# The delta rule's token-tile loop written out as straight-line code on TensorE, VectorE, ScalarE and GpSimd

## The reference, cut to what matters

```python
q = q / (norm(q) + EPS); k = k / (norm(k) + EPS)        # 16 heads of 64
alpha = sigmoid(h @ alpha_w + alpha_b); beta = sigmoid(h @ beta_w + beta_b)
def step(s, inp):
    qt, kt, vt, at, bt = inp
    s = s * at[..., None]
    u = einsum('bhd,bhdv->bhv', kt, s)
    s = s + bt[..., None, None] * (kt[..., None] * (vt - u)[..., None, :])
    return (s, einsum('bhdv,bhd->bhv', s, qt))
```

## Time and profile before

| | us |
|---|---|
| median of three runs | 3277.32 |
| lowest and highest of the three | 3269.51, 3278.38 |
| the profiled execution, own time | 3278.78 |
| its span (first to last instruction) | 3277.0 |
| PE busy | 2846.8 (87%) |
| DVE, ACT, POOL busy | 1550.5 (47%), 1069.3 (33%), 510.5 (16%) |
| the eight tiles of the delta rule | about 2351 to 2905 |

### The profile page before, as it was taken

How to read it: one execution, slowest core, us unless ns; L and a number is a source line. 1 busy time by engine, 2 the same in 40 slices (tenths; PEclk the granted TensorE clock), 3 DMA queues, 4 the chain that set the end, 5 groups by cost and what they waited for, 6 DMA issues and landing times. The chain is left out here.

```text
span 3277.0 us, 97385 instructions
## 1 busy us (share of the span) xinstructions
PE 2846.8 (87%) x43492; PEld 1948.6 (59%) x43492; DVE 1550.5 (47%) x2617; ACT 1069.3 (33%) x1482; POOL 510.5 (16%) x430
## 2 busy tenths in 40 slices
PE   7999999999968799989999999998698999877254
PEld 4666666666645566646666666665477777744132
DVE  3535353535445511145454454544554455524987
ACT  2333333333322121124434344343345444421111
POOL 2333333333312200010000000000011111100000
PEclk8999999999975599989999999998799999988577
DMA  2101110111000001021111111110100000010000
GB/s 78 38 27 38 27 37 27 34 30 32 12 12 0 17 36 38 26 99 37 30 40 27 37 32 32 38 27 30 44 3 4 3 3 3 4 40 29 0 0 13
DMA packets 48769, 88.92 MB, mean 27 GB/s; under 512 B 8640, under 2 KB 43264, under 8 KB 46976
## 3 DMA queue, kind: packets, MB, share of 16 engines
q1 hardware_dynamic: 48384, 82.96, 8.3%
HBM read 81.90 MB, written 1.05 MB: 25 GB/s over the span
## 5 line engine op out<-in xcount | busy, mean ns | idle before, releaser
L525 DVE TENSOR_REDUCE x_mx<-banks 128x2 f32<-128x800 f32 (+1 forms) x512 | 507.0, 993 | 306.3 <-PE banks L640 218.1
L726 PE MATMUL banks<-x_wv,x_cT 128*128 128x256 f32 (+1 forms) x1664 | 467.5, 404 | 24.1 <-DVE x_nmb L530 21.1
L584 PE MATMUL banks<-x_cT,x_wk 128*128 128x400 f32 (+1 forms) x1024 | 364.1, 511 | 17.6 <-DMA x_cT<-in_ctx 17.6
L726 PEld LDWEIGHTS banks<-x_wv,x_cT 128*128 128x128 f32 (+1 forms) x1664 | 279.8, 186 | 146.0 <-issue 76.3
L433 ACT ACTIVATE x_PT<-banks,x_kbs 128x1024 f32<-128x1024 f32 (+1 forms) x208 | 231.5, 1113 | 377.2 <-PE banks L692 377.2
L433 ACT ACTIVATE x_PT<-banks 128x1024 f32<-128x1024 f32 (+1 forms) x208 | 212.8, 1023 | 430.1 <-PE banks L692 358.4
L692 PE MATMUL banks<-x_qbd,x_kT 32*128 32x128 f32 x6656 | 294.7, 274 | 0.0
L584 PEld LDWEIGHTS banks<-x_cT,x_wk 128*128 128x128 f32 x1024 | 193.3, 192 | 163.6 <-issue 27.8
L678 PE MATMUL banks<-x_PT,x_V 128*32 128x64 f32 x13312 | 272.1, 222 | 20.7 <-ACT x_PT L433 20.7
L692 PEld LDWEIGHTS banks<-x_qbd,x_kT 32*128 32x128 f32 x6656 | 253.7, 183 | 0.0
L678 PEld LDWEIGHTS banks<-x_PT,x_V 128*32 128x32 f32 x13312 | 204.9, 109 | 73.7 <-ACT x_PT L433 25.8
(11 more groups left out here) (319 smaller groups left out, 4111.0 us busy)
## 6 DMA issues: line engine op xcount, KB each, us to landing
x_cT<-in_ctx SPq DMA_DIRECT2D x96, 400.0 KB, 3.7
x_cT<-in_ctx SPq DMA_DIRECT2D x32, 401.0 KB, 3.6
e_wu<-in_mo_up SPq DMA_DIRECT2D x9, 512.0 KB, 3.7
e_wd<-in_mo_down SPq DMA_DIRECT2D x9, 512.0 KB, 4.5
x_mrow<-in_mask_row SPq DMA_DIRECT2D x1, 3202.0 KB, 11.5
g_w<-in_db_w SPq DMA_DIRECT2D x3, 1024.0 KB, 7.8
d_wqk<-in_db_qk SPq DMA_DIRECT2D x1, 2048.0 KB, 7.4
f_wgu<-in_fp_gu SPq DMA_DIRECT2D x1, 1536.0 KB, 6.4
```

What stands on the lines that cost most here:

```text
L525: dve.reduce_max(mx[:, H0[k]:H0[k] + 3:2, kb], g.PS[:, first:first + 2, 0:KBS[kb]], AXX).then_inc(max_read, 1)
L584: last = pe.matmul(PJ[pb][:, 0:KBS[k]], wk[:, c, gg, :], cT[:, (p + 1) % 2, c, KB0[k]:KB0[k] + KBS[k]], start=c == 0, stop=c == KC - 1)
L726: last = pe.matmul(PJ[pb][0:CHK[c], 0:D], cT[:, p, cc, 128 * c:128 * c + CHK[c]], wv[:, cc, :], start=cc == 0, stop=cc == KC - 1)
```

## The change

The four `with loop(...)` statements of the delta rule become Python loops. On PE, DVE and ACT the six passes (i = 0 to 5) are written out as tiles 1 to 6, on POOL the seven passes as tiles 0 to 6. The tile's number is then a constant everywhere: in every wait's count, and in the few slices that are picked by the tile (`bass.ds(t, 1)` of `gate`, `beta` and `XN`, and `bass.ds(128 * t, 128)` of `hcT`). The order of the instructions on each engine, their shapes, buffers and semaphores stay as they are.

```diff
@@ -1685,7 +1685,7 @@
             next_tile(0)
-            with loop(nc, pool, NT - 1) as t:
+            for t in range(NT - 1):
                 tile(t, False)
             tile(NT - 1, True)
@@ -1812,7 +1812,7 @@
             levels(0, False, True)
-            with loop(nc, act, NT - 2) as i:
+            for i in range(NT - 2):
                 levels(i + 1, True, True)
             levels(NT - 1, True, False)
@@ -1967,7 +1967,7 @@
             levels(0, False, True)
-            with loop(nc, dve, NT - 2) as i:
+            for i in range(NT - 2):
                 levels(i + 1, True, True)
             levels(NT - 1, True, False)
@@ -2167,7 +2167,7 @@
             levels(0, False, True)
-            with loop(nc, pe, NT - 2) as i:
+            for i in range(NT - 2):
                 levels(i + 1, True, True)
             levels(NT - 1, True, False)
```

## The result

The changed kernel takes 3268.32 us (median of 20 runs, 3261.54 to 3276.99), the kernel before 3275.97 us (20 runs on the same chips): 7.7 us less, a ratio of 0.998 with a 95% interval of 0.9971 to 0.9988. That is inside the 0.3% which I had called no change, and clear of zero.

The account below looks back on a forecast made before the run. PE's instruction stream was taken to set the pace, with missing instruction packets from level 2 on. Terms -2.8 - 1.6 - 2.1 = -6.5 us took 3277.3 to 3270.8 us; range 3264 to 3284.

Parts of the forecast that it names:

- the exit's: PE's fall-through from the loop into tile 7: its 2.06 us stop goes when written out, -2.1 us; 0 if it moves.
- The long stretch: PE from level 2 to L2036, tiles 1 to 6: 31.31 us falls to tile 0's 30.85, -2.8 us in all.
- The stretch ahead: PE from the q projection to level 2: cheaper waits kept, 17.47 to 17.20 us a tile, -1.6 us in all.
- 3. and 4.: Value projection to next tile's transposes, and a tile's first 14 us: nothing taken for either.
- 6.: DVE, ACT and POOL lose register instructions and branch, but their work stays under PE: nothing; +3 us if one stalled.
- the signs for tiles: Profile after: tile starts 67.2 to 67.5 us apart and 13 to 14 instruction packets per tile.
- Rival B: Saved waits kept in full, 2.1 us per tile x 6 + 2.1 = 14.7 us, 3262.6 us; chance 0.08.
- Rival C: Written-out code gets packets at tile 7's slower pace: long stretch +10.2 us, +6.5 in all, 3283.8 us; chance 0.15.
- Rival D: Long stretch gains nothing, the passes' mean being raised by two slow ones: -3.7 us, 3273.6 us; chance 0.22.

Follow-up runs that it names:

- PE alone: Kernel before with only PE's six passes written out; DVE, ACT and POOL keep their loops: 3270.36 us against 3275.30, ratio 0.9984.
- the folded one: Changed kernel with a hardware loop of a single pass around PE's six tiles, its counter folded to a constant: 3267.96 us, ratio 0.9977 to the kernel before.
- the shifted one: Changed kernel with 128 semaphore counts on PE ahead of the delta rule, moving later code half a packet: 3275.41 us against 3271.17 before, ratio 1.0011.
- The two passes with register waits: Changed kernel, but PE loops twice over three written-out tiles, with tile numbers from a register: 3289.65 us against 3281.58 for the kernel before, ratio 1.0021.
- the run without the hint: Kernel before with the branch hint left out of PE's loop (`hint_back_edge=False`): 3284.50 us, ratio 1.0027.
- doubled waits: Changed kernel with every PE wait in levels 2 to 4 made twice: 3284.03 us, ratio 1.002 to the kernel before.
- the shifted loops: Kernel before, loops kept, with 128 semaphore counts on PE ahead of the delta rule, moving later code half a packet: 3298.75 us, ratio 1.0045.

## Why the prediction was right, point by point

The forecast was 3270.8 us, 6.5 us less than before; 3268.3 and 7.7 less were measured. The bound, the engine that counts and the sign of every term were right. One term was too large, the exit's, and the largest one may have been too small.

1. The long stretch, forecast -0.46 us a tile from tile 0 alone. The profile after has -0.85. A tile scatters by over 1 us, and one sample was too few. Taking all tiles at full clock with constants (six of the changed kernel, four of PE alone, five of the folded one, six of the shifted one, mean 30.7 us) against the eighteen with the loop's old cut (mean 31.5), it is -0.8 a tile, about -5 us in all instead of -2.8. But this leaves out three slow tiles with a clock dip, all on the constants' side. With them the mean is 31.0 and the difference -0.55, -3.3 us in all, near the forecast. Which of the two is right stays open: the dips stand behind packet gaps and may belong to the constants. The mechanism holds: I had put all that the waits could give back at 2.1 us a tile; in tile 2's long stretch alone they gave back 2.3, and missing packets took 1.4 of them.
2. The stretch ahead: forecast -0.27, measured 17.47 to 17.19, -0.28, in every tile. The two passes with register waits keep 17.46 to 17.53, so it is the constants.
3. and 4. Nothing, and nothing: the first 14.33 us of a tile are 14.33 after (2432.73 - 2418.40), and the end behind L2036 is 66.90 - 14.33 - 17.19 - 30.24 = 5.14 us in tile 1, 66.47 - 14.33 - 17.19 - 30.11 = 4.84 in tile 2.
5. The exit: the stop of 2.06 us went, as forecast, and the run without the hint shows that the hint had put it there. The fear that it might only move did not come true here; it moves where the loop stays and the cut changes. "Nothing of tile 7 catches it up" was wrong: 0.8 us came back in a packet gap of level 1, so it is worth 1.3 in that window.
6. DVE, ACT and POOL: nothing, and the run with these three alone excludes a gain of more than 2 us.

With item 1 at -3.3 to -5.1 us the sum by measured terms is -6.3 to -8.1 us, beside 7.7 between the medians. Of the signs for tiles, the distance of their starts missed: 66.47 to 67.43 us, mean 66.9, for the forecast 67.2 to 67.5. The two spans differ by more, 9.7 us, and the terms account for -6.5 in tiles 1 to 6 and -1.3 at tile 7's start. The rest lies in code that didn't change and was in no sum: the delta rule's first transpose comes 2.5 us earlier (2348.95 for 2351.45), tile 0 takes 0.9 more (69.45 for 68.56), tile 7's second window 1.4 less, and what follows it 1.1 more. One profile of each kernel can't tell a term of 1 us in a single place, and that the forecast came within 1.2 us of the medians is in part luck.

Rival B (the waits kept in full) fell: it asked for 14.7 us, and doubled waits cost 0.045 us each. Rival C is the instructive one. Its reason, that the packets' pace depends on where the code is cut, is shown; the sign was the wrong way round. I had feared that written-out code would lose the loop's cut. It did lose it, and the loop's cut was better than two others by 2.2 us a pass in the profiles (1.2 by the ratios of the shifted loops); but with constants even the less lucky cut is below the loop's 31.31 (30.46 and 30.99). Rival D (item 1 is nothing, 3.7 us in all) lies just outside the interval of the measured gain, 3.9 to 9.5 us, so it fell, though not by much.

What stays open is why one cut is so much better than another, and whether it matters more with register waits. In their profiles the shifted loop and the two passes of three both have 33.5 us, and only the old cut has 31.3. A packet that holds both a projection and many waits could be the difference; no run here moved one without the other.

## What to carry to other kernels

Where a kernel's own trace already has written-out and looped copies of the same function, compare them stretch by stretch before costing anything: it gave the engine, the sign and the stop at the exit. Gaps in the middle of a run of matmuls, with no wait near them and a whole number of packets apart, are missing instructions; where they stood here, a cheaper wait was worth a third to a half of its price, and the remedy was fewer instructions (covered waits left out, another 0.2 to 0.3%). And a difference of 0.2 to 0.4% between two versions of such a kernel can be no more than the places at which the code is cut: shift it by half a packet before believing in it.

## What the runs showed of the hardware that I had not expected

A missing packet can cost more than its gap. In the run with PE alone written out, tile 1 took 33.42 us in the long stretch where others took 30. Four windows of it:

```profile
2446.07:2459.00 12.93, 10.94 (x485) 10.20 (x488) 7.80 (x19) 8.60 (x17) 2.56 (x4) 1.00 0.02 4
2459.00:2462.60 3.60, 1.88 (x69) 1.70 (x64) 0.40 (x2) 1.52 (x4) 0.00 (x0) 0.98 0.02 5
2462.60:2466.00 3.40, 3.40 (x39) 3.06 (x39) 0.00 (x0) 1.25 (x5) 0.00 (x0) 0.52 0.00 0
2466.00:2479.49 13.49, 10.95 (x444) 10.27 (x436) 5.77 (x10) 8.04 (x15) 0.00 (x0) 1.00 0.02 4
```

PE was busy for 1.88 of 3.60 us, with a packet gap of 1.8 us in it, and then the granted clock was 0.52, the 1.2 GHz level, for the next 3.4 us, in which a matmul of the alpha projection takes 0.42 us, and 0.28 in tile 2. The kernel before and the changed one had no such dip in tiles 1 to 6 of their profiles, so it is no part of their difference there (both have one in tile 7); but in the other kernels the tiles at a clock of 0.95 or less were the slowest or among them. In all of them the dip starts 0.2 to 2 us behind a gap of 1.5 to 2.3 us in the weight loads. But the changed kernel's gap of 1.50 us in tile 2 has none behind it. That the gap brings the dip on is argued from its place, and no run was made for it.

The loop of one pass had constant waits and no register instruction at them, so a test of register waits needs at least two passes.
